# Window attention and a 3x3 convolution on one core: the projection's matmul operands and the path of the softmax reciprocals

## The chip, the cores and the metric

One core of one Trainium2 chip. The metric is the device time of one execution, in microseconds. The kernel before has a median of 3646.91 us over 3 runs (3644.57 to 3647.12).

## The reference

The input is x, 32 images of 56 x 56 positions with 128 channels, fp32. Two residual blocks follow each other:

```python
x = x + L0(_gn(x), qkv_weight, qkv_bias, proj_weight, proj_bias, rel_pos_table)
x = x + L1(_gn(x), w, pruning_mask)
```

_gn is a group norm over 32 groups of 4 channels. L0 is shifted window attention: the image is rolled by 3 positions and cut into 8 x 8 windows of 7 x 7 = 49 tokens; q, k and v are made for 8 heads of 16 channels; the scores get a bias by relative position (and a mask in the windows at the edges); softmax over 49 tokens; times v; then the projection

```python
attn = jax.nn.softmax(attn, axis=-1)
x = jnp.einsum('whnm,whmd->whnd', attn, v).transpose(0, 2, 1, 3).reshape(B * nW, N, C)
x = x @ proj_weight.T + proj_bias
```

L1 is a 3 x 3 convolution, 128 to 128 channels, with binarized weights. All is fp32 in the reference.

## The kernel before, in words

**Layout.** Channels lie on the 128 partitions. An image is worked on in 8 rows of windows (ROWS); a row has 8 windows of 49 tokens, 392 tokens in all (RT). The four pairs of heads (PAIRS) of a row are four units, so an image has 32 units (UNITS), and the kernel has 32 x 8 = 256 rows and 1024 units.

**The order of work.** There is no planner: each engine's program is written out, `for i in images: for u in range(32)`, with fixed places (units) for every job: VALUES_AT = 5, NORMED_AT = 8, SPLIT_AT = 9, PROJ_AT = 9 and so on, plus multiples of 4 for each next row. An engine runs its own list strictly in order and waits on semaphores. Attention of image i, the convolution of image i-1 and the loading and first norm of image i+1 run interleaved in the same loop.

**One unit of attention.** PE computes scores (L908) for a pair of heads; DVE adds the bias (L766, s_sb) and takes the maximum (L771); POOL subtracts it (L443); ACT takes Exp (L498, probs); PE transposes (L919, two units later); ACT copies the result from PSUM (L505, probsT). With all four units of a row there, PE runs the value matmuls (L932), and with head_ones the sums of the probabilities (L936), into attn_ps; both are written column group by column group. These come at unit 5 of a row.

**The reciprocals.** The sums lie 98 columns wide (two windows of 49) on partition 16 h + 4 a + copy, for head h, window pair a (SUM_PARTS = 4) and four equal copies. At unit 6 DVE takes the reciprocal (L746). SP then sends the 32 rows with copy 0 to DRAM (L366, recip_dram), waits for it to land, and reads them back so that each head's 392 values reach its 16 channels' partitions (L371, recip_wide). At unit 8 DVE multiplies (L751, o_sb). SP's queue holds also the loads of x (L378, x_in) and the stores (L383, out_dram).

**The split and the projection.** ACT makes oT_hi, o_sb in fp16 (L548, unit 8, before q in ACT's queue). DVE makes oT_lo = o_sb - oT_hi in fp16 (L759, at the head of unit 9, before that unit's bias add). PE multiplies at the end of unit 9 with the helper `three` (L895): hi x hi, hi-weight x lo, lo-weight x hi, into misc_ps, just before the next row's value matmuls. DVE then adds the result to x (L809) and takes norm statistics (L815). misc_ps is one PSUM bank, shared by the projection, the transposes of x in (L975) and out (L981) and the group norm's small matmuls (L992, fp32, 128 x 128 weights with 2 columns).

qkv (L895 also), with fp16 halves, and the convolution (L1014) use the same high and low scheme; the change leaves them.

Of the kernel before, what the change touches and what calls it, by code (L numbers as in the profile page):

```python
# [31 lines left out]
ALU = mybir.AluOpType  # L32
ACT = mybir.ActivationFunctionType
AX = mybir.AxisListType
F32 = mybir.dt.float32
F16 = mybir.dt.float16
# [37 lines left out]
VALUES_AT, NORMED_AT, SPLIT_AT = 5, 8, 9  # L74
# [88 lines left out]
def build_block(nc, x, wqkv, bqkv, wproj, bproj, table, wconv, prune, ident_d, group_d, parity_d, mask_d, out):  # L163
    with ExitStack() as ctx:
        def sb(name, shape, dt=F32):
            return ctx.enter_context(nc.sbuf_tensor(name, shape, dt))
# [21 lines left out]
        wT_hi = sb("wT_hi", [128, 4, C], F16)  # L188
        wT_lo = sb("wT_lo", [128, 4, C], F16)
# [38 lines left out]
        oT_hi = sb("oT_hi", [128, WIN, W], F16)  # L228
        oT_lo = sb("oT_lo", [128, WIN, W], F16)

        recip_dram = nc.dram_tensor("recip_dram", (2, HEADS, RT), F32).ap()
# [52 lines left out]
        recip_out, recip_wide_in = sem("recip_out"), sem("recip_wide_in")  # L284
        o_ready = sem("o_ready")
        oT_hi_ready, oT_lo_ready = sem("oT_hi_ready"), sem("oT_lo_ready")
# [47 lines left out]
        def _(sp):  # L334
# [24 lines left out]
            def body(i):  # L359
                for u in range(UNITS):  # L360
                    row = row_of(i, u, VALUES_AT + 1)
                    if row is not None:

                        sp.wait_ge(recip_ready, row + 1)
                        need(sp, recip_wide_in, 16 * (row - 1))
                        sp.dma_start(recip_dram[row % 2].rearrange("h (a n) -> (h a) n", a=SUM_PARTS),  # L366
                                     recip[0:128:4, :]).then_inc(recip_out, 16)
                        need(sp, o_ready, row)
                        sp.wait_ge(recip_out, 16 * (row + 1))
                        slot = recip_dram[row % 2]  # L370
                        sp.dma_start(recip_wide[:], bass.AP(tensor=slot.tensor, offset=slot.offset,  # L371
                                                            ap=[[RT, HEADS], [0, HD], [1, RT]]))\
                            .then_inc(recip_wide_in, 16)
# [116 lines left out]
        def _(act):  # L490
# [35 lines left out]
            def body(i):  # L526
                for u in range(UNITS):
# [15 lines left out]
                    row = row_of(i, u, NORMED_AT)  # L543
                    if row is not None:

                        act.wait_ge(o_ready, row + 1)
                        need(act, oT_lo_ready, row)
                        nc.scalar.copy(flat(oT_hi), flat(o_sb)).then_inc(oT_hi_ready, 1)  # L548
# [47 lines left out]
        def _(dve):  # L596
# [49 lines left out]
            step(vec.tensor_copy(w_f[:, 3, :], misc_ps[:, 0:C]))  # L646
            step(vec.tensor_copy(wT_hi[:], w_f))
            step(vec.tensor_tensor(wT_lo[:], w_f, wT_hi[:], ALU.subtract))
# [89 lines left out]
            def body(i):  # L738
                for u in range(UNITS):

                    row = row_of(i, u, VALUES_AT + 1)
                    if row is not None:

                        dve.wait_ge(attn_ready, row + 1)
                        need(dve, recip_out, 16 * row)
                        vec.reciprocal(recip[:], attn_ps[:, RT:RT + SUM_COLS]).then_inc(recip_ready, 1)  # L746
                    row = row_of(i, u, NORMED_AT)
                    if row is not None:

                        dve.wait_ge(recip_wide_in, 16 * (row + 1))  # L750
# [4 lines left out]
                    row = row_of(i, u, SPLIT_AT)  # L755
                    if row is not None:

                        dve.wait_ge(oT_hi_ready, row + 1)
                        vec.tensor_tensor(flat(oT_lo), flat(o_sb), flat(oT_hi), ALU.subtract).then_inc(oT_lo_ready, 1)  # L759
# [114 lines left out]
        def _(pe):  # L874
# [94 lines left out]
            def misc(i, u, kind, t):  # L969
# [12 lines left out]
                if kind == "proj":  # L982
                    pe.wait_ge(oT_lo_ready, i * ROWS + (t + 1 if u >= PROJ_AT else t + 1 - ROWS))
                    hi, lo = (o[:].rearrange("p r w -> p (r w)") for o in (oT_hi, oT_lo))
                    last = three(misc_ps[:, 0:RT], ((wT_hi[:, 3, :], hi), (wT_hi[:, 3, :], lo), (wT_lo[:, 3, :], hi)))
# [109 lines left out]
```

## Time and profile before

| | us |
|---|---|
| median of 3 runs | 3646.91 |
| the profiled execution | 3636.98 |
| its span, first to last instruction | 3635.2 |
| PE busy | 3190.5 (88%) |
| DVE busy | 3073.1 (85%) |
| ACT busy | 2555.1 (70%) |
| POOL busy | 2365.1 (65%) |

The span is the time between the first and the last instruction of the execution that the profiler recorded. Busy shares are of that span. PE is TensorE's matmuls, whose ends are modelled; PEld is its weight loads, which run beside them. SP issues DMAs, and SPq is its queue. An idle time is put down to the instruction or DMA whose semaphore came last. The granted clock of TensorE was 0.983 of full speed over the span.

### The profile page before, as it was taken

What the parts mean: (1) busy time and instruction counts of PE and PEld (TensorE: products, weight loads), DVE (VectorE), ACT (ScalarE), POOL (GpSimd) and SP (SyncE); (2) the same over time, 40 slices, a digit from 0 to 9 for tenths busy, and PEclk for the clock granted to TensorE, in tenths of its full rate; (3) what the DMA queues carried; (4) which work ended last, traced back from release to release, by engine and by line L of the source; (5) the groups of instructions that cost most, each with busy time, mean ns of one, the idle gap of its engine ahead of it and who ended that gap; (6) DMA issues with size and microseconds to landing.
All of it is one profiled execution on the core that took longest, in us unless ns stands there. A gap on an engine that the chain in (4) does not pass through costs nothing.

```text
span 3635.2 us, 155064 instructions
## 1 busy us (share of the span) xinstructions
PE 3190.5 (88%) x64395; PEld 2684.8 (74%) x64395; DVE 3073.1 (85%) x6399; ACT 2555.1 (70%) x5729; POOL 2365.1 (65%) x3683
## 2 busy tenths in 40 slices
PE   2889989889899899898899999889898899898896
PEld 1667777777777777777777777777777777787775
DVE  5689888888888888888888888888888898888895
ACT  1667777767677777777777777777677777777772
POOL 4466666766667666667766667766667666667763
PEclk9999999999999999999999999999999999999998
DMA  2111111111111111111111111111111111111111
GB/s 57 37 42 52 47 42 47 49 50 49 37 47 50 49 52 47 42 47 50 52 52 50 42 45 49 50 52 50 37 47 50 50 52 47 42 47 50 34 35 36
DMA packets 260489, 169.26 MB, mean 47 GB/s; under 512 B 23120, under 2 KB 259792, under 8 KB 259792
## 3 DMA queue, kind: packets, MB, share of 16 engines
q1 hardware_dynamic: 259792, 159.34, 15.9%
q8 instruction: 514, 8.42, 1.0%
q14 instruction: 183, 1.50, 0.1%
HBM read 104.69 MB, written 54.59 MB: 44 GB/s over the span
## 4 chain that ended last, share of the span: by engine, by line
PE 33%; DVE 32%; issue 13%; POOL 9%; DMA 8%; ACT 4%; SPq 0%; DVEq 0%; ACTq 0%; POOLq 0%
PE conv_ps L1014 8%; DVE s_sb L766 6%; PE qkv_ps L895 6%; DMA recip_wide<-recip_dram 5%; PE attn_ps L932 4%; PE scores_ps L908 4%; PE attn_ps L936 4%; DVE plane_lo L778 3%; POOL s_sb L443 3%; DVE s_max L771 3%; DMA recip_dram<-recip 3%; DVE oT_lo L759 3%; PE probsT_ps L919 3%; DVE tok_lo L856 3%; DVE recip L746 2%
## 5 line engine op out<-in xcount | busy, mean ns | idle before, releaser
L443 POOL TENSOR_TENSOR s_sb<-s_sb,s_max 113x392 f32<-113x392 f32 x1024 | 998.9, 975 | 1092.7 <-DVE s_max L771 1091.4
L505 ACT COPY probsT<-probsT_ps 128x392 f32<-128x392 f32 x1024 | 490.8, 479 | 376.6 <-PE probsT_ps L919 366.4
L498 ACT ACTIVATE probs<-s_sb 113x392 f32<-113x392 f32 x1024 | 552.4, 539 | 221.1 <-POOL s_sb L443 218.6
L470 POOL TENSOR_TENSOR plane<-x_n 128x224 f32<-128x224 f32 x896 | 656.4, 753 | 18.7
L919 PE MATMUL probsT_ps<-ident,probs 113*128 113x113 f32 x4096 | 585.0, 265 | 38.7 <-ACT probsT L505 35.3
L771 DVE TENSOR_REDUCE s_max<-s_sb 113x8 f32<-113x392 f32 x1024 | 574.9, 561 | 35.3
L766 DVE TENSOR_TENSOR s_sb<-scores_ps,bias 113x392 f32<-113x392 f32 x1024 | 565.8, 552 | 41.0 <-PE scores_ps L908 37.1
L569 ACT COPY v<-qkv_ps 64x256 f32<-64x256 f32 (+2 forms) x1280 | 391.0, 325 | 211.6 <-PE qkv_ps L895 205.5
L1014 PE MATMUL conv_ps<-plane_hi,wc_hi 128*128 128x224 f16 x2688 | 484.4, 263 | 23.1 <-DVE conv_y L840 19.0
L919 PEld LDWEIGHTS probsT_ps<-ident,probs 113*128 113x128 f32 x4096 | 433.5, 141 | 90.7 <-ACT probs L498 47.9
L908 PE MATMUL scores_ps<-k,q 32*49 32x98 f32 x16384 | 477.4, 252 | 19.7 <-issue 19.4
L1014 PE MATMUL conv_ps<-plane_hi,wc_lo 128*128 128x224 f16 x2688 | 479.4, 261 | 0.0
L1014 PE MATMUL conv_ps<-plane_lo,wc_hi 128*128 128x224 f16 x2688 | 410.1, 262 | 34.9 <-DVE plane_lo L778 34.9
L908 PEld LDWEIGHTS scores_ps<-k,q 32*49 32x49 f32 x16384 | 365.6, 121 | 90.4 <-issue 32.6
L895 PE MATMUL qkv_ps<-wT_hi,tok_hi 128*128 128x128 f16 (+1 forms) x2304 | 395.6, 226 | 3.7 <-ACT v L569 1.9
L895 PE MATMUL qkv_ps<-wT_hi,tok_lo 128*128 128x128 f16 (+1 forms) x2304 | 389.1, 220 | 1.7 <-issue 1.7
L895 PE MATMUL qkv_ps<-wT_lo,tok_hi 128*128 128x128 f16 (+1 forms) x2304 | 389.1, 220 | 0.4 <-issue 0.3
L932 PEld LDWEIGHTS attn_ps<-probsT,v 128*32 128x32 f32 x16384 | 208.5, 113 | 218.5 <-ACT probsT L505 190.6
L932 PE MATMUL attn_ps<-probsT,v 128*32 128x49 f32 x16384 | 244.8, 213 | 129.7 <-ACT probsT L505 128.8
L482 POOL TENSOR_SCALAR x_n<-x,gn_y,gn_shift 128x371 f32<-128x371 f32 (+2 forms) x576 | 347.4, 613 | 7.6 <-POOL gn_shift L432 7.6
L746 DVE RECIPROCAL recip<-attn_ps 128x98 f32<-128x98 f32 x256 | 195.7, 765 | 162.9 <-PE attn_ps L936 162.6
L560 ACT ACTIVATE k<-qkv_ps,k_bias,k_scale 128x392 f32<-128x392 f32 x512 | 322.9, 687 | 4.5 <-PE qkv_ps L895 4.4
(144 smaller groups left out, 6799.1 us busy)
## 6 DMA issues: line engine op xcount, KB each, us to landing
x_in<-in_x_dram SPq DMA_DIRECT2D x224, 224.0 KB, 3.9
recip_wide<-recip_dram SPq DMA_DIRECT2D x256, 196.0 KB
out_dram<-x_out SPq DMA_DIRECT2D x224, 224.0 KB, 2.3
recip_dram<-recip SPq DMA_DIRECT2D x256, 12.2 KB, 1.7
x<-in_L_conv_w_dram SPq DMA_DIRECT2D x1, 576.0 KB
x<-L_conv_pruning_mask_dram SPq DMA_DIRECT2D x1, 576.0 KB
x_n<-_conv_rel_pos_table_dram SPq DMA_DIRECT2D x14, 10.7 KB
x_n<-in_mask_dram SPq DMA_DIRECT2D x1, 196.0 KB
```

The lines of the kernel that those rows point to most:

```text
L443: nc.gpsimd.tensor_tensor(s, s, top, ALU.subtract).then_inc(sub_ready, 1)
L470: last = nc.gpsimd.tensor_tensor(plane[:, t % 2, j], *sums[j])
L498: nc.scalar.activation(probs[0:QP, slot % 2, :, :, 0:N], s_sb[0:QP, slot % 4], ACT.Exp)\
L505: nc.scalar.copy(probsT[:, g % PT_SLOTS], probsT_ps[:].rearrange("p (w n) -> p w n", n=ODD)[:, :, 0:N])\
L569: last = nc.scalar.copy(v[half, slot, w0:w0 + n, :, e * HD:(e + 1) * HD], vals[half, b:b + n, :, e, :])
L766: vec.tensor_tensor(s_sb[0:QP, u % 4].rearrange("p w h m -> p (w h m)"), scores_ps[0:QP, u % 2, 0:WP * 2 * N], bias[0:QP, edge, u % PAIRS] ...
L771: vec.tensor_reduce(s_max[0:QP, u % 4], s_sb[0:QP, u % 4].rearrange("p w h m -> p (w h) m"), AX.X, ALU.max).then_inc(max_ready, 1)
L895: last = mm(out_ps, w, t, start=(n == 0), stop=(n == 2))
L908: last = mm(scores_ps[p0:p0 + N, (u + n) % 2, (w // 2) * 2 * N:(w // 2 + 1) * 2 * N], q[at, r % 2, w, :], k[at, r % 2, w].rearrange("p e m ...
L919: last = nc.tensor.transpose(probsT_ps[:, w * 128:w * 128 + QP], probs[0:QP, u % 2, w].rearrange("p e m -> p (e m)"), ident[0:QP, 0:QP])
L932: mm(attn_ps[parts, w * N:(w + 1) * N], v[:, row % 2, w, pair, :], probsT[:, (row * PAIRS + pair) % PT_SLOTS, w, :], start=True, stop=True)
L1014: last = mm(conv_ps[:, j, 0:PP].rearrange("p (r w) -> p r w", w=W), w[:, j * KW + dx, :], p[:, j, k * TPAIRS:(k + 1) * TPAIRS, dx:dx + W], ...
```

## The change

The fp16 halves of the attention output (oT_hi, oT_lo) are gone, with ACT's and DVE's instructions for them and their semaphores. The projection is one matmul of fp32 weights (w_proj) with o_sb; it waits for o_ready where it waited for oT_lo_ready, at the same place of PE's program. The DRAM tensor for the reciprocals and the DMA into it are gone. In their place four DMAs, one for each window pair a, read recip on the 8 partitions 4 a + 16 h, each with a step of 0 and a count of 16, and write 98 columns of all 128 partitions of recip_wide. SP waits before them for the reciprocal and for o_sb of the row before. DVE's reciprocal waits for the four DMAs of the row before where it waited for the DMA to DRAM. The once-only setup casts three weight matrices to fp16 halves where it cast four.

```diff
--- before.py
+++ after.py
@@ -71,7 +71,7 @@
 
 
 LAG_T = 2
-VALUES_AT, NORMED_AT, SPLIT_AT = 5, 8, 9
+VALUES_AT, NORMED_AT = 5, 8
 MID, END = 0, 1
 PROJ_AT = 9
 G2_JOBS = ((6, END), (7, MID))
@@ -185,8 +185,9 @@
         parity = sb("parity", [128, 2])
         three_halves, zero = sb("three_halves", [128, 1]), sb("zero", [128, 1])
         b_in = sb("b_in", [128, 4])
-        wT_hi = sb("wT_hi", [128, 4, C], F16)
-        wT_lo = sb("wT_lo", [128, 4, C], F16)
+        wT_hi = sb("wT_hi", [128, 3, C], F16)
+        wT_lo = sb("wT_lo", [128, 3, C], F16)
+        w_proj = sb("w_proj", [128, C])
         head_ones = sb("head_ones", [128, SUM_PARTS, 2 * HD])
         w_max = sb("w_max", [128, 4])
         w_inv = sb("w_inv", [128, 4])
@@ -225,10 +226,6 @@
         recip = sb("recip", [128, SUM_COLS])
         recip_wide = sb("recip_wide", [128, RT])
         o_sb = sb("o_sb", [128, WIN, W])
-        oT_hi = sb("oT_hi", [128, WIN, W], F16)
-        oT_lo = sb("oT_lo", [128, WIN, W], F16)
-
-        recip_dram = nc.dram_tensor("recip_dram", (2, HEADS, RT), F32).ap()
 
         class Norm:
 
@@ -281,9 +278,8 @@
         probsT_sb = sem("probsT_sb")
         attn_ready = sem("attn_ready")
         recip_ready = sem("recip_ready")
-        recip_out, recip_wide_in = sem("recip_out"), sem("recip_wide_in")
+        recip_wide_in = sem("recip_wide_in")
         o_ready = sem("o_ready")
-        oT_hi_ready, oT_lo_ready = sem("oT_hi_ready"), sem("oT_lo_ready")
         head_consts = sem("head_consts")
         scaled_bias_ready = sem("scaled_bias_ready")
         tok_hi_ready, tok_lo_ready = sem("tok_hi_ready"), sem("tok_lo_ready")
@@ -362,15 +358,11 @@
                     if row is not None:
 
                         sp.wait_ge(recip_ready, row + 1)
-                        need(sp, recip_wide_in, 16 * (row - 1))
-                        sp.dma_start(recip_dram[row % 2].rearrange("h (a n) -> (h a) n", a=SUM_PARTS),
-                                     recip[0:128:4, :]).then_inc(recip_out, 16)
                         need(sp, o_ready, row)
-                        sp.wait_ge(recip_out, 16 * (row + 1))
-                        slot = recip_dram[row % 2]
-                        sp.dma_start(recip_wide[:], bass.AP(tensor=slot.tensor, offset=slot.offset,
-                                                            ap=[[RT, HEADS], [0, HD], [1, RT]]))\
-                            .then_inc(recip_wide_in, 16)
+                        for a in range(SUM_PARTS):
+                            sp.dma_start(recip_wide[:, a * SUM_COLS:(a + 1) * SUM_COLS],
+                                         recip[SUM_PARTS * a:128:HD, :].unsqueeze(1).to_broadcast((HEADS, HD, SUM_COLS)))\
+                                .then_inc(recip_wide_in, 16)
                     for kind, t in misc_at(i, u):
                         if kind == "tin" and live(i, 2):
 
@@ -540,12 +532,6 @@
                                 .then_inc(m1_ready, 1)
                     if live(i, 0 if u >= LAG_T else -1):
                         evacuate_probsT(i, i * UNITS + (u - LAG_T), u - LAG_T)
-                    row = row_of(i, u, NORMED_AT)
-                    if row is not None:
-
-                        act.wait_ge(o_ready, row + 1)
-                        need(act, oT_lo_ready, row)
-                        nc.scalar.copy(flat(oT_hi), flat(o_sb)).then_inc(oT_hi_ready, 1)
                     misc(i, u, MID)
                     r, j = divmod(u, PAIRS)
                     if live(i, 0 if r < ROWS - 1 else 1):
@@ -643,9 +629,9 @@
             step(vec.tensor_scalar(w_in[:, 3, :], misc_ps[:, 0:C], w_inv[:, 3:4], None, ALU.mult))
             dve.sem_inc(proj_scaled, 1)
             dve.wait_ge(setup_pe, 4)
-            step(vec.tensor_copy(w_f[:, 3, :], misc_ps[:, 0:C]))
-            step(vec.tensor_copy(wT_hi[:], w_f))
-            step(vec.tensor_tensor(wT_lo[:], w_f, wT_hi[:], ALU.subtract))
+            step(vec.tensor_copy(w_proj[:], misc_ps[:, 0:C]))
+            step(vec.tensor_copy(wT_hi[:], w_f[:, 0:3, :]))
+            step(vec.tensor_tensor(wT_lo[:], w_f[:, 0:3, :], wT_hi[:], ALU.subtract))
 
             step(vec.tensor_scalar(q_scale[:], w_max[:, 0:1], HD ** -0.5, None, ALU.mult))
             step(vec.tensor_scalar(q_bias[:], b_in[:, 0:1], HD ** -0.5, None, ALU.mult))
@@ -742,21 +728,16 @@
                     if row is not None:
 
                         dve.wait_ge(attn_ready, row + 1)
-                        need(dve, recip_out, 16 * row)
+                        need(dve, recip_wide_in, 16 * SUM_PARTS * row)
                         vec.reciprocal(recip[:], attn_ps[:, RT:RT + SUM_COLS]).then_inc(recip_ready, 1)
                     row = row_of(i, u, NORMED_AT)
                     if row is not None:
 
-                        dve.wait_ge(recip_wide_in, 16 * (row + 1))
+                        dve.wait_ge(recip_wide_in, 16 * SUM_PARTS * (row + 1))
                         vec.tensor_tensor(o_sb[:].rearrange("p r (w c) -> p w r c", c=WIN),
                                           attn_ps[:, 0:RT].rearrange("p (w r c) -> p w r c", r=WIN, c=WIN),
                                           recip_wide[:].rearrange("p (w r c) -> p w r c", r=WIN, c=WIN), ALU.mult)\
                             .then_inc(o_ready, 1)
-                    row = row_of(i, u, SPLIT_AT)
-                    if row is not None:
-
-                        dve.wait_ge(oT_hi_ready, row + 1)
-                        vec.tensor_tensor(flat(oT_lo), flat(o_sb), flat(oT_hi), ALU.subtract).then_inc(oT_lo_ready, 1)
                     if live(i):
 
                         g = i * UNITS + u
@@ -980,9 +961,8 @@
                     for s in range(SUB):
                         last = nc.tensor.transpose(misc_ps[0:SP_, s * C:(s + 1) * C], result[:, s * SP_:(s + 1) * SP_], ident[:])
                 if kind == "proj":
-                    pe.wait_ge(oT_lo_ready, i * ROWS + (t + 1 if u >= PROJ_AT else t + 1 - ROWS))
-                    hi, lo = (o[:].rearrange("p r w -> p (r w)") for o in (oT_hi, oT_lo))
-                    last = three(misc_ps[:, 0:RT], ((wT_hi[:, 3, :], hi), (wT_hi[:, 3, :], lo), (wT_lo[:, 3, :], hi)))
+                    pe.wait_ge(o_ready, i * ROWS + (t + 1 if u >= PROJ_AT else t + 1 - ROWS))
+                    last = mm(misc_ps[:, 0:RT], w_proj[:], flat(o_sb), start=True, stop=True)
                 if kind in ("gn1", "gn2"):
                     gn, img = (gn1, i + 1) if kind == "gn1" else (gn2, i - 1)
                     if t == 0:
```

## Rows read from the trace of the kernel before

**Rows 1.** The page, part 1: busy us (share of span) and instructions, by engine.

```profile
...
PE 3190.5 (88%) x64395; PEld 2684.8 (74%) x64395; DVE 3073.1 (85%) x6399; ACT 2555.1 (70%) x5729; POOL 2365.1 (65%) x3683
...
```

**Rows 2.** The page, part 4: the chain that ended last, by engine and by line.

```profile
...
PE 33%; DVE 32%; issue 13%; POOL 9%; DMA 8%; ACT 4%; SPq 0%; DVEq 0%; ACTq 0%; POOLq 0%
PE conv_ps L1014 8%; DVE s_sb L766 6%; PE qkv_ps L895 6%; DMA recip_wide<-recip_dram 5%; PE attn_ps L932 4%; PE scores_ps L908 4%; PE attn_ps L936 4%; DVE plane_lo L778 3%; POOL s_sb L443 3%; DVE s_max L771 3%; DMA recip_dram<-recip 3%; DVE oT_lo L759 3%; PE probsT_ps L919 3%; DVE tok_lo L856 3%; DVE recip L746 2%
...
```

**Rows 3.** Waits, whole span: who waited for whom, us in total, times, longest us.

```profile
...
DVE recip L746 <- PE attn_ps L936: 162.6, 105, 4.3
PE attn_ps L932 <- ACT probsT L505: 128.8, 69, 3.4
...
DVE o_sb L751 <- DMA recip_wide<-recip_dram: 103.0, 78, 3.5
DVE x L809 <- PE misc_ps L895: 50.5, 61, 1.5
...
ACT oT_hi L548 <- DVE o_sb L751: 38.6, 75, 8.5
...
PE qkv_ps L895 <- ACT q L557: 26.9, 42, 3.0
...
PE misc_ps L895 <- DVE oT_lo L759: 23.5, 56, 2.6
...
```

**Rows 4.** The chain from 1500 to 1560 us: start us, us, what.

```profile
...
1531.96 0.78 DVE recip L746
1532.76 1.69 DMA recip_dram<-recip
1534.51 4.20 DMA recip_wide<-recip_dram
...
1541.78 0.39 PE probsT_ps L919 x4
...
```

**Rows 5.** Timeline of DVE, 1529 to 1546: start, us, line, shapes, [idle before].

```profile
...
1538.73 0.57 DVE L751 TENSOR_TENSOR o_sb<-attn_ps,recip_wide 128x392 f32<-128x392 f32 x1 [2.18 <-DMA recip_wide<-recip_dram]
...
1541.18 1.20 DVE L759 TENSOR_TENSOR oT_lo<-o_sb,oT_hi 128x392 f16<-128x392 f32 x1
...
```

**Rows 6.** Groups by line and shape: count, busy us, mean ns, idle before.

```profile
...
L759 DVE TENSOR_TENSOR oT_lo<-o_sb,oT_hi 128x392 f16<-128x392 f32 x256 | 223.9, 874 | 2.3 <-ACT oT_hi L548 2.2
...
L548 ACT CAST oT_hi<-o_sb 128x392 f16<-128x392 f32 x256 | 133.2, 520 | 44.5 <-DVE o_sb L751 38.6
...
L992 PE MATMUL misc_ps<-gn_mv,group 128*128 128x2 f32 x128 | 22.1, 242 | 31.2 <-DVE gn_mv L702 16.5 <-ACT x_out L522 12.9 <-DVE gn_mv L706 1.7
...
L992 PEld LDWEIGHTS misc_ps<-gn_mv,group 128*128 128x128 f32 x128 | 19.6, 193 | 38.3 <-ACT x_out L522 19.3 <-issue 18.9
...
```

**Rows 7.** Timeline of PE, 1541 to 1546: the projection.

```profile
...
1543.39 0.33 PE L895 MATMUL misc_ps<-oT_hi,wT_hi 128*128 128x392 f16 x1
1543.56 0.33 PE L895 MATMUL misc_ps<-oT_lo,wT_hi 128*128 128x392 f16 x1
...
```

**Rows 8.** Timeline of PE, same stretch: head_ones matmuls and what follows.

```profile
...
1544.72 0.85 PE L936 MATMUL attn_ps<-probsT,head_ones 128*32 128x98 f32 x32
1545.50 0.72 PE L908 MATMUL scores_ps<-k,q 32*49 32x98 f32 x24
```

**Rows 9.** Timeline of all engines, 1500 to 1516: second DMA and o_sb.

```profile
...
1510.20 0.61 SPq L371 DMA_DIRECT2D recip_wide<-recip_dram  x1
...
1513.50 0.57 DVE L751 TENSOR_TENSOR o_sb<-attn_ps,recip_wide 128x392 f32<-128x392 f32 x1 [0.36 <-DMA recip_wide<-recip_dram]
...
```

**Rows 10.** Timeline of SP, 0 to 14 us: loads at the start.

```profile
...
0.72 0.42 SPq L345 DMA_DIRECT2D ident<-in_ident_dram  x1
1.20 0.41 SPq L345 DMA_DIRECT2D group<-in_group_dram  x1
...
```

**Rows 11.** DMA queues, 1510.2 to 1513.5: packets, MB, share of 16 engines.

```profile
...
q1 hardware_dynamic: 136, 0.20, 18.9%
...
```

**Rows 12.** DMA queues, 1508.4 to 1510.2 us.

```profile
...
q1 hardware_dynamic: 48, 0.01, 3.0%
...
```

## The prediction, made before the changed kernel was run

> **What bounds the kernel now.** I read the engine totals first: in the profiled execution PE is busy 88% of the span, VectorE (DVE) 85%, ScalarE (ACT) 70% [rows 1]. No engine is full, so the second view is the chain of waits: PE holds 33% of the chain, DVE 32%, DMA 8% [rows 2]. PE and DVE carry it by turns. Third, the list of waits says where they hand over [rows 3]. PE stands 128.8 us before the value matmuls (L932) for ScalarE's copy of probsT, and 26.9 and 23.5 us for ACT's q and for DVE's oT_lo. DVE stands 162.6 us before the reciprocal for those same value matmuls, 103.0 us (78 of 256 rows) before o_sb (L751) for the DMA into recip_wide, and 50.5 us before L809 for the projection. The loop over one image row of windows (256 in all, 3635.2 / 256 = 14.2 us each) is: reciprocal, DMA to DRAM, DMA back, o_sb, then at the same place of DVE's queue the scores' bias add and maximum, POOL's subtraction, ACT's Exp and probsT copy, PE's value matmuls, reciprocal. The chain between 1500 and 1560 us shows one pass in which 0.78 us of L746, 1.69 us of the first DMA and 4.20 us of the second follow each other [rows 4]; o_sb then started after 2.18 us in which DVE stood still, and the oT_lo of that row took 1.20 us of DVE one unit on [rows 5].
>
> **The change part by part**, against the profiled execution's own 3636.98 us (span 3635.2; the median of the three runs, 3646.91, is 10 us more, which is added at the end).
>
> *oT_lo on DVE goes.* 256 x 874 ns = 223.9 us of DVE work [rows 6]. The chain names L759 for 3% of the span, 0.03 x 3635 = 109 us [rows 2]; the other 115 us lay beside other work. L759 stands at the head of unit 1 of each row, before that unit's bias add and maximum, so these come earlier, and through POOL and ACT so does the probsT copy for which PE stands 128.8 us. But a little later in the same units DVE waits for PE already (L809 and L746, 50.5 + 162.6 = 213 us [rows 3]): a DVE that arrives earlier waits there unless PE is earlier too. Bounds: -224 us to 0. I take 60% of the chain's 109: **-65 us**, as PE's own waits of 128.8 and 23.5 us are of that size.
>
> *oT_hi on ACT goes.* 256 x 520 ns = 133.2 us of ACT work and 38.6 us of standing for o_sb [rows 3, 6]. It stands before q in ACT's queue, and PE waits 26.9 us for q. The chain's largest lines do not name L548. Bounds -39 to 0; I take a little over half of PE's wait for q: **-15 us**. ACT is the least loaded of the three, so the rest is cover already.
>
> *The projection: three fp16 matmuls become one fp32.* The three start 0.17 us apart (the first two stand in the rows), so they hold PE for 3 x 0.17 = 0.50 us [rows 7]. No full-width fp32 matmul of 392 columns is in the trace. What is there: the 64 gn matmuls (128x128 weights, fp32, two per image) leave 128 records, that is two weight loads (193 ns each) and two matmuls for each, so a full-width fp32 product is run as two [rows 6]. And a moving fp32 column costs two clocks: the 32 head_ones matmuls of 98 columns, four column groups beside each other, hold PE from 1544.72 to 1545.50; 0.78 us / (8 x 98) = 1.0 ns a column; the transposes of 113 columns, four in 0.39 us, 0.86 ns a column [rows 4, 8]. So 2 x 392 x 0.86 = 0.68 us, and of the 193 ns of the first weight load up to 0.1 us more shows than of an fp16 one. Against 0.50 that is +0.18 to +0.28 us a row; I take 0.22, x 256 = **+56 us**, all of it on the path, since with a lighter DVE and ACT it is PE that the others wait for. Bounds: run once like a transpose, 0.34 - 0.50 = -0.16 us a row, -41 us; four times, 4 x 0.34 - 0.50 = +0.86 us, +220 us. I keep the middle as the gn rows are nearest. The result also lands later for L809: a matmul record lasts about 0.16 us beyond its columns, the same as before, so the added wait of DVE is these 0.22 us and not more.
>
> *The two DMAs through DRAM become four from SBUF to SBUF.* Before: from the start of the first issue (1532.76) to that of the second (1534.51) 1.75 us; from there to o_sb, in a row beside no x_in load, 3.3 us (the issue at 1510.20, and at 1513.50 o_sb, which had waited for it) [rows 9]. That is 5.05 us. After: SP issues four in line. The recip_wide issue, which has the same 8 x 16 shape, holds SP 0.61 us, and the start-up loads in one queue follow each other by 0.48 us [rows 9, 10]; so the fourth starts 3 x 0.48 = 1.4 us to 3 x 0.66 = 2.0 us after the first, and I take 2.0. It must then land: the 12 KB DMA took 1.69 us [rows 4], and here 128 packets of 392 B leave on 8 of the 16 engines. (The DMA of 128 rows left 136 packets, 8 beyond its rows, that of 32 rows 48, 16 beyond: one closing packet per engine used [rows 11, 12].) A packet of 392 B took 0.030 x 16 x 1.8 us / 48 = 18 ns, one of 1568 B 0.189 x 16 x 3.3 / 136 = 73 ns; 16 packets per engine are 0.3 us. So 2.0 + 1.7 + 0.3 = 4.0 us, 1.05 us before the old path. Bounds: issues every 0.48 us and a landing of 1.7 us, 3.1 us in all (1.9 us sooner); issues every 0.66 us and a landing as slow as recip_wide's 4.20 us of [rows 4], 6.2 us (1.15 us later). The gain counts only in the 78 rows in which DVE stood for it, and at most what it stood, 1.3 us on average: I take 78 x 0.6 = **-45 us**; bounds -103 and, later by 1.15 us in 78 rows, +90. SP's own queue is no worse: it was held 1.75 + 0.61 = 2.4 us per row by the two steps, and is held 4 x 0.64 = 2.6 us by the four, so x_in and out_dram issues move by 0.2 us, which have units of slack. The reciprocal's new wait is for a DMA that o_sb of the row before has already waited for, so it costs nothing.
>
> The packets argue against splitting only mildly. The Trainium skill (DMA: Bandwidth & Descriptors, Rules for kernel authors) says that small transfers are to be merged, since below 64 KB one pays mostly overhead; the four have 49 KB each, and its fixed cost of some 2 us (section Anatomy of one DMA, given for GpSimd's path), if paid four times in line, makes an estimate of 8 us. The start-up rows [rows 10] show issues every 0.48 us without waiting for the landing, so by this trace the overheads overlap; taken strictly, the rule is the slow rival below.
>
> Sum: -65 - 15 + 56 - 45 = **-69 us**, 3637 - 69 = 3568 for the profiled execution, **3578 us** as a median.
>
> **The rivals.**
> *A: PE takes all.* PE has 3190.5 / 256 = 12.5 us of work in a row of 14.2 [rows 1]. If the waits of DVE and ACT merely swap into waits for PE, the -65 and -15 shrink to the 23.5 us that PE stood for oT_lo, the DMA gain to 20, and +56 stays: about +12 us, 3659 (-20 to +15). For it: the 213 us that DVE already waits for PE. Against it: PE stands 129 us for probsT, behind DVE's work.
> *B: the loop opens.* The issues are short (3.1 us path), the removed L759 stops holding POOL and the fp16 casts, and PE's waits for probsT, q and oT_lo (179 us) all go together with 60 us elsewhere; less 56: -183, about 3465. For it: DMA and DVE lie in one loop. Against it: the 85% of DVE only falls to 79%.
> *C: slower, by the four transfers.* One mechanism: the fourth transfer lands 6.5 us or more after the reciprocal, as the repeated reads of one partition and four closings hold the same 8 engines, worst when an x_in load is in flight. DVE reaches o_sb two units (half a row, 7.1 us) after the reciprocal when nothing holds it; a landing near that makes nearly every row wait. At 7 us: 2 us more than now in 78 rows and 0.5 in half of the others, 156 + 45 = +200, less what DVE's lighter load gives (-80) plus PE's 56: about +176, 3820; at 6.2 us +90 - 80 + 56 = +66, 3713. The decisive point is a landing 0.3 us later than now, at 5.4 us, where 78 x 0.3 cancels the other terms' -24. The same side is reached if the fp32 product runs as four (+220 in place of +56: +95, 3742).
> *That it does not do what it says:* the 8 x 16 repeat could be run as other packets than 128 per DMA; then it is C.
>
> **How the numbers follow.** Chances: forecast (-20 to -130 us) 0.55; A 0.15; B 0.12; C 0.18. The range takes all of the forecast's and part of each rival: 3510 to 3665. 0.2% is 7 us, what this kernel's measurement can tell. Faster: 0.55 + 0.12 + a quarter of A = 0.71; same 0.08, of A; slower 0.18 + the rest of A = 0.21.
>
> **What would show it.** Two records per projection, of some 0.5 us, starting 0.34 us apart; more or fewer refutes that step. SP's four issues with 0.6 us each; the fourth's landing 4.0 us after the first's start. DVE's wait for recip_wide under 60 us in total; no L759, L548; DVE near 2850 us busy; PE's wait for probsT down by a third or more, and DVE's wait for the value matmuls up. If PE's share stays at 88% of a shorter span and probsT's wait is unchanged, the -65 was wrong. If DVE's wait for recip_wide rises, C holds.

## The result, and the profile after

The changed kernel takes 3518.76 us (median of 4 runs, 3518.06 to 3519.10), the kernel before 3645.74 us beside it. The ratio is 0.9659, 95% interval 0.9637 to 0.9681: 3.4% faster, some 124 us. The forecast was 3578 us, in the range 3510 to 3665. The direction and the mechanism's main part came out, with a size 1.8 times that forecast. The kernel before scatters from 3623 to 3658 us over all runs, so the ratios below, each against runs of it beside the kernel, say more than its median; they were run in four groups, in which the kernel before has medians of 3642.7, 3633.9, 3645.9 and 3653.0 us.

The page of the changed kernel, parts 1 and 4, answering to [rows 1] and [rows 2]:

```profile
...
PE 3193.4 (91%) x64139; PEld 2678.4 (76%) x64139; DVE 2897.2 (82%) x6143; ACT 2448.0 (70%) x5473; POOL 2302.2 (65%) x3683
...
```

```profile
...
PE 45%; DVE 21%; POOL 18%; issue 11%; ACT 2%; SPq 1%; DMA 1%; DVEq 0%; POOLq 0%; ACTq 0%
PE conv_ps L994 11%; PE qkv_ps L876 8%; PE scores_ps L889 7%; POOL s_sb L435 6%; PE attn_ps L913 5%; DVE s_sb L747 5%; PE probsT_ps L900 5%; PE attn_ps L917 4%; POOL plane L462 4%; PE misc_ps L965 3%; DVE plane_lo L759 3%; DVE s_max L752 2%; POOL x_n L451 2%; PE misc_ps L956 1%; POOL gn_t L419 1%
...
```

PE has the same busy time in a span 118.9 us shorter: its idle time fell from 3635.2 - 3190.5 = 444.7 us to 3516.3 - 3193.4 = 322.9 us, by 121.8. That is the gain as the page counts it, but not all of its causes: the fp32 product puts 46 us of new work into the 3193.4 us (worked out below), so PE's other work, the same instructions as before, took some 43 us less. Part of that is a higher clock, which e2 below shows. PE went from 33% of the chain to 45%, DVE from 32 to 21, DMA from 8 to 1. DVE's busy time fell by 175.9 us, and not by oT_lo's 223.9 (plane_lo took 14 us more; the rest wasn't traced), to 82%.

The changed kernel's waits, answering to [rows 3] (who waited for whom: us, times, longest us):

```profile
...
DVE recip L732 <- PE attn_ps L917: 196.1, 132, 4.4
DVE x L790 <- PE misc_ps L965: 177.8, 191, 2.6
PE attn_ps L913 <- ACT probsT L497: 143.9, 98, 3.6
...
DVE o_sb L737 <- DMA recip_wide<-recip: 30.4, 44, 2.5
...
PE misc_ps L965 <- DVE gn_mean L697: 16.2, 31, 0.6
...
PE qkv_ps L876 <- ACT q L543: 3.7, 2, 3.0
...
PE scores_ps L889 <- issue: 0.9, 2, 0.5
...
PE conv_ps L994 <- DVE plane_lo L759: 0.9, 1, 0.9
...
PE misc_ps L965 <- DVE o_sb L737: 0.6, 1, 0.6
...
```

Three of these had no row ahead of the prediction. The kernel before has, in the waits of PE:

```profile
...
PE conv_ps L1014 <- DVE plane_lo L778: 34.9, 31, 2.4
PE misc_ps L895 <- DVE gn_mean L711: 30.4, 30, 1.0
...
PE scores_ps L908 <- issue: 19.4, 23, 1.3
...
```

Of PE's 122 us the reader finds 34.0 at the convolution's wait for plane_lo (34.9 to 0.9), 22.9 at the projection's wait for oT_lo (23.5, now 0.6 for o_sb), 23.2 at q (26.9 to 3.7), 18.5 before the scores (19.4 to 0.9) and 14.2 at gn_mean (30.4 to 16.2), 113 us together; two waits for ACT's x_out, 12.9 and 11.1 us, are gone too. The wait for probsT, from which the prediction drew its largest term, did not fall: 128.8 became 143.9 us. DVE's waits for PE grew: before the reciprocal 162.6 to 196.1 us, before L790 (the old L809) 50.5 to 177.8. For recip_wide DVE stands 30.4 us in 44 rows, where it was 103.0 in 78.

The projection and POOL's subtraction by line and form (count, busy us, mean ns, idle before), answering to the rows of L895 and L443:

```profile
...
L435 POOL TENSOR_TENSOR s_sb<-s_sb,s_max 113x392 f32<-113x392 f32 x1024 | 959.9, 937 | 1037.2 <-DVE s_max L752 1036.4
...
L965 PE MATMUL misc_ps<-o_sb,w_proj 128*128 128x392 f32 x512 | 218.6, 509 | 17.9 <-DVE gn_mean L697 16.2 <-ACT x L506 1.2 <-DVE o_sb L737 0.6
...
L965 PEld LDWEIGHTS misc_ps<-o_sb,w_proj 128*128 128x128 f32 x512 | 77.7, 191 | 34.0 <-DVE gn_mean L697 24.3 <-ACT x_out L514 5.7 <-ACT x L506 2.5
...
```

```profile
...
1548.59 0.84 PE L965 MATMUL misc_ps<-o_sb,w_proj 128*128 128x392 f32 x2
1549.36 0.93 PE L913 MATMUL attn_ps<-probsT,v 128*32 128x49 f32 x64
...
```

In the kernel before the three fp16 matmuls start at 1543.39 [rows 7], and the value matmuls at:

```profile
...
1543.98 0.91 PE L932 MATMUL attn_ps<-probsT,v 128*32 128x49 f32 x64
...
```

Each of the 256 projections has two records of some 0.5 us, which start 0.35 us apart (the median of all), and the value matmuls start 0.77 us after the first; before it was 0.59 us. Both figures are also the medians of all rows in which PE did not wait in between. So the product costs PE 0.18 us a row, 46 us.

The four DMAs of one row: the timeline of SP, and the DMA engines from 1511 to 1515 us in 40 slices of 0.1 us (busy tenths, then the queue's packets, MB and share):

```profile
...
1511.05 2.52 SPq L363 DMA_DIRECT2D recip_wide<-recip  x4
...
```

```profile
...
DMA  0000000000000343443334434349343334434320
...
q1 hardware_dynamic: 544, 0.20, 25.8%
...
```

Four issues in 2.52 us, packets from 1.3 to 3.9 us after the first began, 544 = 4 x 136 packets, which by the prediction's count (128 rows and one packet for each engine) is 8 engines again. A packet took 0.258 x 16 x 4 us / 544 = 30 ns. In the 44 rows in which DVE stood for recip_wide, o_sb began 4.2 to 6.0 us after the first issue, 4.3 in the median; before it was 4.9 to 7.6, 5.5 in the median. The path is about 4 us long, as forecast, and some 1.2 us shorter than before.

### The profile page after: what moved, and what is told of

Same layout as the page of the kernel before. It is cut to its first block, busy times and chain, and to the rows that moved or that the text cites. A ratio compares the mean times of both kernels' runs of the same rounds, so it can differ in the third digit from the quotient of the medians.

```text
span 3516.3 us, 154043 instructions
## 1 busy us (share of the span) xinstructions
PE 3193.4 (91%) x64139; PEld 2678.4 (76%) x64139; DVE 2897.2 (82%) x6143; ACT 2448.0 (70%) x5473; POOL 2302.2 (65%) x3683
## 4 chain that ended last, share of the span: by engine, by line
PE 45%; DVE 21%; POOL 18%; issue 11%; ACT 2%; SPq 1%; DMA 1%; DVEq 0%; POOLq 0%; ACTq 0%
PE conv_ps L994 11%; PE qkv_ps L876 8%; PE scores_ps L889 7%; POOL s_sb L435 6%; PE attn_ps L913 5%; DVE s_sb L747 5%; PE probsT_ps L900 5%; PE attn_ps L917 4%; POOL plane L462 4%; PE misc_ps L965 3%; DVE plane_lo L759 3%; DVE s_max L752 2%; POOL x_n L451 2%; PE misc_ps L956 1%; POOL gn_t L419 1%
## 5 line engine op out<-in xcount | busy, mean ns | idle before, releaser
L435 POOL TENSOR_TENSOR s_sb<-s_sb,s_max 113x392 f32<-113x392 f32 x1024 | 959.9, 937 | 1037.2 <-DVE s_max L752 1036.4
L462 POOL TENSOR_TENSOR plane<-x_n 128x224 f32<-128x224 f32 x896 | 639.7, 734 | 18.7
L889 PE MATMUL scores_ps<-k,q 32*49 32x98 f32 x16384 | 458.9, 248 | 0.9 <-issue 0.9
L889 PEld LDWEIGHTS scores_ps<-k,q 32*49 32x49 f32 x16384 | 353.7, 119 | 65.1 <-issue 7.1
L913 PE MATMUL attn_ps<-probsT,v 128*32 128x49 f32 x16384 | 245.7, 214 | 146.2 <-ACT probsT L497 143.9
L732 DVE RECIPROCAL recip<-attn_ps 128x98 f32<-128x98 f32 x256 | 196.2, 766 | 196.3 <-PE attn_ps L917 196.1
L790 DVE SCALAR_TENSOR_TENSOR x<-misc_ps,w_max,x 128x371 f32<-128x371 f32 (+2 forms) x576 | 199.7, 393 | 178.2 <-PE misc_ps L965 177.8
L474 POOL TENSOR_SCALAR x_n<-x,gn_y,gn_shift 128x371 f32<-128x371 f32 (+2 forms) x576 | 333.9, 590 | 7.6 <-POOL gn_shift L424 7.6
```

Of the source, the lines that this page charges most:

```text
L435: nc.gpsimd.tensor_tensor(s, s, top, ALU.subtract).then_inc(sub_ready, 1)
L462: last = nc.gpsimd.tensor_tensor(plane[:, t % 2, j], *sums[j])
L889: last = mm(scores_ps[p0:p0 + N, (u + n) % 2, (w // 2) * 2 * N:(w // 2 + 1) * 2 * N], q[at, r % 2, w, :], k[at, r % 2, w].rearrange("p e m ...
L913: mm(attn_ps[parts, w * N:(w + 1) * N], v[:, row % 2, w, pair, :], probsT[:, (row * PAIRS + pair) % PT_SLOTS, w, :], start=True, stop=True)
```

## The experiments

All times are medians; "of before" is the ratio with its 95% interval.

| run | us | of before |
|---|---|---|
| changed kernel | 3518.8 | 0.9659 (0.9637 to 0.9681) |
| e1: the DMAs alone | 3616.8 | 0.9926 (0.9900 to 0.9952) |
| e3: the fp32 matmul alone, halves still made | 3640.2 | 0.9999 (0.9985 to 1.0012) |
| e2: fp32 matmul, no halves, reciprocals by DRAM | 3532.6 | 0.9702 (0.9675 to 0.9729) |
| e4: changed, subtraction back at its place | 3609.4 | 0.9914 (0.9892 to 0.9936) |
| e8: changed, subtraction late in the unit | 3586.6 | 0.9881 (0.9855 to 0.9907) |
| e9: changed, multiply twice | 3612.9 | 0.9908 (0.9878 to 0.9938) |
| e5: changed, ACT's copy back | 3521.4 | 0.9699 (0.9678 to 0.9720) |
| e6: changed, projection twice | 3625.5 | 0.9982 (0.9968 to 0.9997) |
| e11: changed, tok_lo moved to POOL | 3518.5 | 0.9655 (0.9630 to 0.9680) |
| e10: changed, reciprocals of 49 columns by DRAM | 3654.3 | 1.0025 (1.0008 to 1.0043) |
| e7: changed, projection one unit earlier | 3719.9 | 1.0247 (1.0192 to 1.0301) |
| e12: changed, values and reciprocal first | 3764.9 | 1.0319 (1.0293 to 1.0345) |

### The parts by themselves: e1, e3, e2

e1 is before with SP's four DMAs in place of its two.

> The kernel before with the four SBUF-to-SBUF DMAs alone; the fp16 halves and their three matmuls stay. Theory D (the DMA path carries the gain: DVE's standing for recip_wide fell from 103.0 to 30.4 us, and that loop paces the rows): about 80 us under before, some 3565. Theory V (DVE's removed oT_lo carries it, at the head of unit 1 before the scores' bias add): about 35 us under before, some 3610, and DVE's wait for recip_wide still falls below 40 us.

e3 is before with

```diff
-  last = three(misc_ps[:, 0:RT], ((wT_hi[:, 3, :], hi), (wT_hi[:, 3, :], lo), (wT_lo[:, 3, :], hi)))
+  last = mm(misc_ps[:, 0:RT], w_proj[:], flat(o_sb), start=True, stop=True)
```

> The kernel before with the fp32 matmul in the place of the three fp16 ones; ACT and DVE still make both halves, and PE still waits for oT_lo, though nothing reads them; reciprocals through DRAM. This is the price of the matmul alone. If PE's time there is on the path in full: 0.18 us x 256 = 46 us over before, some 3690. If it is covered by PE's waits for probsT: 0 to +15 us.

e2 is the changed kernel with SP's two DMAs through DRAM.

> The changed kernel with the reciprocals again through DRAM in two DMAs; one fp32 matmul, no halves. Theory V: 90 to 100 us under before, 3545 to 3555, as oT_lo's 224 us of DVE are gone. Theory D: 30 to 50 us under before, about 3605, with DVE's wait for recip_wide at 100 us or more.

The three make a ladder: before 1, the matmul 0.9999, the halves gone 0.9702, the DMAs 0.9659. In us of some 3640: 0, then -108, then -16. The last step is not clear of the noise: the intervals of e2 and of the changed kernel overlap (0.9675 and 0.9681). So theory V holds and D falls. Alone, on the kernel before, the DMAs give 27 us (0.9926; 17 to 36 by the interval). e1's waits show that they did their work and yet gave little:

```profile
...
PE attn_ps L926 <- ACT probsT L499: 143.3, 89, 3.8
...
DVE o_sb L745 <- DMA recip_wide<-recip: 38.7, 39, 2.4
...
```

DVE's wait for recip_wide fell by 64 us, and 14.5 us of it came back as PE's wait for probsT (128.8 to 143.3).

The matmul cost nothing, though it was there. Part 1 of the page of e3, and one of its waits:

```profile
...
PE 3238.2 (89%) x64139; PEld 2703.1 (74%) x64139; DVE 3085.2 (85%) x6400; ACT 2551.0 (70%) x5729; POOL 2360.3 (65%) x3683
...
```

```profile
...
PE attn_ps L934 <- ACT probsT L506: 112.8, 66, 3.1
...
```

PE is 47.7 us busier than before (3238.2 against 3190.5), as 256 x 0.18 = 46 says, in the same time: its idle time gave it, 16 us of that the wait for probsT.

The page of e2, parts 1 and 4, and one of its waits:

```profile
...
PE 3195.7 (90%) x64139; PEld 2678.5 (76%) x64139; DVE 2902.9 (82%) x6143; ACT 2447.9 (69%) x5473; POOL 2300.3 (65%) x3683
...
PE 49%; DVE 21%; issue 9%; POOL 9%; DMA 8%; ACT 3%; SPq 0%; DVEq 0%; ACTq 0%; POOLq 0%
...
```

```profile
...
DVE o_sb L742 <- DMA recip_wide<-recip_dram: 88.4, 76, 3.1
...
```

Here DMA still holds 8% of the chain and DVE stands 88.4 us for recip_wide, and the kernel is only some 15 us slower than the changed one. A wait of 88 us is not a price of 88 us.

Not all of the 108 us between e3 and e2 was waiting. Both run the same 64139 matmuls, and PE is 42.5 us less busy in e2 (3195.7 against 3238.2). Its mean granted clock is higher:

```profile
...
core 0: 3640.2 us, clock 0.979
...
core 0: 3534.0 us, clock 0.988
...
```

(e3, then e2.) The clock has two levels, 1.0 (2.4 GHz) and 0.5 (1.2 GHz), and the mean says how long it stood at the lower one: 2 x 0.021 x 3640 = 153 us in e3, 2 x 0.012 x 3534 = 85 us in e2. At the lower level matmuls take twice as long (rows below), so at most half of the difference, 34 us of the 108, came back with the clock (an estimate). The scatter of one kernel agrees: e1 took 3598.7 us in the run with 0.986 and 3627.6 in one with 0.977. One fall in the kernel before, with the 14 us ahead of it (us, then PE, PEld, DVE, ACT and POOL busy, granted clock, DMA):

```profile
...
977.42:991.42 14.00, 10.23 (x231) 8.05 (x230) 8.93 (x17) 10.08 (x24) 12.41 (x28) 1.00 0.24 67
991.42:994.84 3.42, 3.42 (x19) 1.83 (x20) 2.29 (x5) 2.54 (x6) 3.32 (x5) 0.50 0.02 5
...
```

```profile
...
993.67 0.53 PE L895 MATMUL misc_ps<-oT_hi,wT_hi 128*128 128x392 f16 x1
994.00 0.53 PE L895 MATMUL misc_ps<-oT_lo,wT_hi 128*128 128x392 f16 x1
...
```

PE had been busy for 10.23 of 14.00 us, 73% where its share of the span is 88%, and was then held at the lower level while it worked: the projection's matmuls start 0.33 us apart there, where they start 0.17 us apart at the full clock [rows 7]. Ahead of the other 25 falls between 100 and 3450 us of that trace it was busy 66 to 80%. The kernel before was granted 0.974 to 0.981 in the runs beside these experiments, the changed kernel 0.986 to 0.988; by the same estimate up to some 40 of its 124 us are this. That fewer stalls of PE are what raised the clock fits these traces but is not shown: e7 below has 0.997 with PE 87% busy.

### What the halves cost, put back one at a time: e4, e5, e8, e9

e4 puts on DVE, at the head of unit 9, with nothing waiting for it:

```diff
+  dve.wait_ge(o_ready, row + 1)
+  vec.tensor_tensor(flat(oT_lo), flat(o_sb), flat(oT_hi), ALU.subtract)
```

> The changed kernel with a subtraction of the same shapes as oT_lo (fp16 <- fp32, fp16 of zeros) put back at the head of unit 9 on DVE; nothing waits for it. Theory V: 60 to 90 us over the changed kernel, 3580 to 3610. Theory D: under 20 us over it, 3519 to 3540, since DVE's added work falls into its 178 us of waiting for the projection.

```profile
...
L748 DVE TENSOR_TENSOR oT_lo<-o_sb,oT_hi 128x392 f16<-128x392 f32 x256 | 209.9, 820 | 0.1
...
```

```profile
...
PE 37%; DVE 29%; POOL 19%; issue 13%; ACT 2%; SPq 1%; DMA 0%; DVEq 0%; POOLq 0%; ACTq 0%
...
```

```profile
...
PE attn_ps L921 <- ACT probsT L499: 175.1, 123, 4.0
...
DVE x L798 <- PE misc_ps L973: 86.3, 95, 2.0
...
PE misc_ps L973 <- DVE gn_mean L700: 45.3, 31, 1.7
...
```

e4 costs 0.9914 - 0.9659 = 2.55% of 3640, 93 us (91 by the medians), for 210 us of DVE. DVE is back at 29% of the chain; PE waits 31 us more for probsT and 29 more for gn_mean, while DVE's wait for the projection halves.

e5 puts `nc.scalar.copy(flat(oT_hi), flat(o_sb))` back on ACT in unit 8; nothing reads the copy, and DVE's next o_sb waits for it.

> The changed kernel with ACT's copy of o_sb to fp16 put back at its old place (unit 8, before q), read by nothing. If ACT's removed work was worth what the prediction said: 15 us over the changed kernel, some 3534, with PE's wait for ACT's q back at 20 us or more. If ACT has cover for all of it: 0 to +5 us. If DVE and ACT removals are worth the same per us of work (the subtraction cost 91 us for its 210): 133 us x 0.43 = +57 us.

```profile
...
PE attn_ps L921 <- ACT probsT L499: 120.9, 94, 3.2
...
PE qkv_ps L884 <- ACT q L550: 21.5, 39, 3.0
...
```

PE does wait 21.5 us for q again (3.7 in the changed kernel), but 23.0 us less for probsT (143.9 there), so the wait mostly moved. The kernel takes 2.6 us more by its median, 0.4% by ratios whose intervals touch. So 133 us of ACT work are worth little; the price is between 3 and 15 us.

e8 has e4's subtraction after the projection's take-up, just ahead of the reciprocal's wait.

> As the kernel with the DVE subtraction put back (91 us over the changed one), but it stands at the end of unit 9's list, after the projection is taken up and just before the reciprocal's wait for PE. If its place ahead of the bias add was what it cost: 0 to 25 us over the changed kernel, 3519 to 3545. If DVE's amount of work counts wherever it stands: 70 us or more over it, 3590 and up.

```profile
...
L849 DVE TENSOR_TENSOR oT_lo<-o_sb,oT_hi 128x392 f16<-128x392 f32 x256 | 168.9, 660 | 0.0
...
```

Between the two expectations, near the second: 0.9881, 81 us (68 by the medians) for 169 us of DVE. The place is worth 10 to 20 us of it. The subtraction takes 660 ns here and 820 ns at the head of the unit.

e9 puts a second multiply ahead of o_sb's:

```diff
+  vec.tensor_tensor(o_twin[:].rearrange(...), attn_ps[:, 0:RT].rearrange(...), recip_wide[:].rearrange(...), ALU.mult)
   vec.tensor_tensor(o_sb[:].rearrange(...), attn_ps[:, 0:RT].rearrange(...), recip_wide[:].rearrange(...), ALU.mult)
```

> The changed kernel with o_sb's multiply run once more just ahead of it, from PSUM into a buffer that nothing reads: 560 ns, 143 us of DVE work of a kind that POOL beside it does not stretch (min 550, max 569 ns). The two subtractions put back (210 and 169 us of DVE) cost 0.43 and 0.40 us per us. If DVE's amount of work is what counts: 143 x 0.42 = 60 us over the changed kernel, some 3579. If it was the contention of an fp16-writing subtraction with POOL: under 20 us over, since POOL's mean for its subtraction stays at 937 ns.

```profile
...
L436 POOL TENSOR_TENSOR s_sb<-s_sb,s_max 113x392 f32<-113x392 f32 x1024 | 969.4, 947 | 1144.3 <-DVE s_max L756 1143.2
...
L738 DVE TENSOR_TENSOR o_twin<-attn_ps,recip_wide 128x392 f32<-128x392 f32 x256 | 142.8, 558 | 29.5 <-DMA recip_wide<-recip 28.4 <-DVE gn_y L721 0.4
...
```

91 us (0.9908) for 143 us of DVE, 0.64 us per us, where 60 us were expected. POOL's subtraction stays at 947 ns (937 in the changed kernel), so it was not contention with POOL. Why this operation costs more for each of its us than the two subtractions is not shown; that it stands ahead of o_sb and so also delays the projection is one candidate. The clock has a part in all three: it was granted 0.982 in e4, 0.983 in e8 and 0.979 in e9, where the changed kernel has 0.988. By the estimate made for e2 that is at most 23, 19 and 34 us of their 93, 81 and 91.

### Who paces the changed kernel: e6, e11

e6 runs `mm(misc_ps[:, 0:RT], w_proj[:], flat(o_sb), start=True, stop=True)` twice.

> The changed kernel with the fp32 projection run twice into the same place (same output): 0.68 us more of PE in each of the 256 rows, 174 us. Theory P (PE paces the changed kernel; DVE waits 178 us for the projection already): +150 to +174 us, some 3680. Theory C (PE's standing of 144 us for probsT covers it, as it covered the dearer matmul in the kernel before, which cost nothing): +40 to +90 us, some 3580.

```profile
...
PE 3365.2 (93%) x64651; PEld 2779.7 (77%) x64651; DVE 2898.3 (80%) x6143; ACT 2447.6 (68%) x5473; POOL 2293.8 (63%) x3683
...
PE 56%; DVE 16%; POOL 16%; issue 9%; ACT 2%; SPq 1%; DMA 1%; DVEq 0%; POOLq 0%; ACTq 0%
...
```

```profile
...
DVE x L790 <- PE misc_ps L966: 328.5, 255, 3.2
...
PE attn_ps L913 <- ACT probsT L497: 80.7, 63, 2.9
...
```

Between the theories: 107 us (118 by ratios) for 172 us of PE, 0.62 per us, at an unchanged clock (0.988). The wait for probsT gave 63 us of cover. The same engine's 46 us cost nothing in the kernel before.

e11 moves the block of tok_lo from DVE's list to the end of POOL's, at the same units.

> The changed kernel with tok_lo's subtraction (DVE, 195 us before) moved to POOL, at the end of the same units. If DVE's work is worth 0.42 us per us and POOL, at 65%, takes it in its waits: 80 us under the changed kernel, some 3440. If POOL's order holds up s_sb (POOL is 18% of the changed kernel's chain): slower than it, 3530 to 3600.

```profile
...
PE 3196.9 (91%) x64139; PEld 2683.2 (76%) x64139; DVE 2752.7 (78%) x5887; ACT 2445.4 (70%) x5473; POOL 2478.9 (71%) x3939
...
PE 53%; POOL 17%; DVE 17%; issue 9%; ACT 2%; SPq 1%; DMA 0%; DVEq 0%; POOLq 0%; ACTq 0%
...
```

Neither came: no change (0.9655). DVE is 144.5 us less busy, POOL 176.7 us more, and PE holds 53% of the chain. More DVE work costs the changed kernel 0.4 to 0.64 us per us; less of it, given to POOL, gains nothing. That would fit a kernel at which the bound passes from DVE to PE, as e6 and PE's 53% suggest. But the edit changed two engines: a gain from DVE can have been eaten by POOL's added work, and no run took work from DVE without giving it to another engine.

### Attempts at a faster version: e10, e7, e12

e10 lays the sums out as 64 rows of one window (`SUM_COLS = N; SUM_PARTS = NWIN`) and carries them through DRAM.

> The changed kernel with the sums laid out on 64 partitions of 49 columns (one window each) in place of 32 of 98, and the reciprocals carried through DRAM in two DMAs. DVE's reciprocal halves, some 385 ns or 98 us less DVE work; head_ones runs as 64 short matmuls for 32. If DVE's work is worth 0.42 us per us: 41 us less than the changed projection with DRAM reciprocals (ratio 0.970 to before), so 0.959, and some 20 us under the changed kernel. If what counts is only the place of oT_lo, or PE: no gain, ratio 0.970 or more.

```profile
...
L923 PE MATMUL attn_ps<-probsT,head_ones 128*32 128x49 f32 x16384 | 249.9, 214 | 15.2 <-issue 15.0
...
L738 DVE RECIPROCAL recip<-attn_ps 128x49 f32<-128x49 f32 x256 | 119.8, 468 | 205.9 <-PE attn_ps L923 205.8
...
```

```profile
...
DVE s_sb L753 <- PE scores_ps L895: 163.7, 237, 2.6
...
```

3.3% slower than e2, which it was made from. The reciprocal took 468 ns and not 385, and DVE then waited 163.7 us for scores. PE runs twice the matmuls for the sums: 16384 head_ones records for 8192, and PE's busy time is 63 us above e2's, at a granted clock of 0.980 for e2's 0.988. Half the columns is not half the time on either engine. How the whole 120 us divides was not measured further.

e7 is `PROJ_AT = 8`.

> The changed kernel with PROJ_AT = 8 for 9: the projection runs a unit earlier on PE, and DVE takes it up a unit earlier, which o_sb of unit 8 allows now that no oT_lo is made at unit 9. If DVE's 178 us of standing for the projection pace the rows: 20 to 60 us under the changed kernel, some 3480. If PE then stands for o_sb, or DVE's wait moves one unit up unchanged: 0 to +40 us.

```profile
...
DVE recip L732 <- PE attn_ps L917: 519.6, 253, 5.8
...
PE misc_ps L962 <- DVE x L790: 227.8, 216, 1.4
...
```

Worse than either expectation, 201 us over the changed kernel. DVE's wait for the projection went (5.4 us are left of 177.8), and PE now stood 227.8 us for DVE to empty misc_ps ahead of the output's transposes: with both jobs at the end of the same unit, the one bank of PSUM passes PE, DVE, PE. That held up the value matmuls, and DVE waits 519.6 us for them. At the old place three units lay between a projection and the next transposes of the output. The clock was not the cause, as it was granted 0.997.

e12 exchanges the order in both lists: on PE `values(row)` ahead of the projection, on DVE the reciprocal ahead of the projection's take-up.

> The changed kernel with the value matmuls ahead of the projection in PE's unit, and DVE's reciprocal ahead of its take-up of the projection (all work kept). The reciprocal, the four DMAs and o_sb then start 0.68 us sooner after the scores, and the projection is off that loop. If the changed kernel is paced by PE's amount of work: the same as the changed kernel, ratio 0.963 to 0.968. If it is the loop over the reciprocal (which a multiply added to it lengthened by 94 us for 143): 256 x 0.68 x 0.4 = 70 us under it, ratio about 0.947. If DVE's bias add of the next unit now comes later behind the projection's take-up: slower than it, 0.97 or more.

```profile
...
DVE recip L775 <- PE attn_ps L917: 693.6, 256, 7.8
...
PE attn_ps L913 <- ACT probsT L497: 286.6, 192, 4.3
...
```

The third expectation held, and more strongly than it was put: 3.2% slower than before. DVE now stands at the reciprocal in all 256 rows, 693.6 us; the projection's take-up and the next bias add stand behind it, and with them the probsT for which PE waits 286.6 us. In the old order the take-up lay in that wait. None of the three beats the changed kernel, and e11 equals it.

## Why the prediction was right, point by point

*oT_lo on DVE (-65 us forecast) and oT_hi on ACT (-15):* together 80, measured 108 by e3 to e2. By e5 3 to 15 of it is ACT's, so DVE's term is 93 to 105: undersized by 1.5. Putting the subtraction back costs 93 (e4), which agrees. The step that set it, 60% of the chain's 109 us, since a DVE that comes earlier "waits there unless PE is earlier too", gave DVE's growing waits too much weight. They did grow, by 161 us, but PE was earlier as well. The forecast also has no term for the clock, of which up to 34 us of the 108 may be made. The bound of 224 was safe. The route was partly wrong: probsT's wait was to fall by a third, and it rose by 12%; the gain came at plane_lo, oT_lo, q, the scores and gn_mean, where DVE's and ACT's whole lists run ahead.

*The fp32 matmul (+56 us, "all of it on the path"):* the amount was right, 0.18 us a row by the traces for 0.22, two records each, 0.5 us long and 0.35 us apart. That it was on the path was the step that failed. On the kernel before it cost 0 us (-5 to +4 by e3's interval). This is the largest error of the sum. The rival that PE takes all had PE's share for it, but e3 shows 46 us covered by PE's own 445 us of idle time, even with the halves still made.

*The DMAs (-45 us):* the path was forecast well, 4.0 us (4.3 in the rows that waited) and fewer than 60 us of waiting (30.4). Its 0.66 us for the slowest issue stands in no row; measured were 0.64. The price was too high: 27 us alone and 16 as the last step, neither of them sharp. Counting 0.6 us for each of 78 waiting rows takes a wait for a price; e2 stood 88 us for the DMA and paid 15. The slow rival, by the small transfers, did not appear: four of 49 KB overlapped, and the 8 us that the prediction names for four overheads in line are twice what the trace shows.

So the sum was wrong in three terms that partly offset: 0 for +56, -108 for -80, -16 for -45, in all -124 for -69. Without the +56 the sum would have been -125, because the errors of the other two cancel; that is luck, as it is that the result lies in the stated range, 9 us from its lower end. What was right for its reason is the sign: DVE's removed work carries the gain.

*Rival A (PE takes all)* does not hold for this gain; for a further one e11 and e6 speak for it without deciding it. *Rival B (-183)* had the right mechanism, PE's waits going together, but counted on probsT's wait, which stayed.

What stays open: why PE's wait for probsT doesn't follow DVE's load (128.8 us before, 143.9 in the changed kernel, 141.6 in e11, 175.1 in e4). What decides the granted clock, and so how the gain divides between waits and clock. Also, what the reciprocals by SBUF are worth on a kernel that PE does not pace.

## What to carry to other kernels

In this kernel two engines each held a third of the chain of waits. Work removed from one, DVE, was worth 0.4 to 0.6 of its duration, and work added to the other, PE, cost nothing at first: 224 us less of DVE gave some 100, and the 46 us on PE cost none. After that 172 us more of PE cost 107, and 145 us less of DVE, moved to POOL, gave 0. When a change has two such parts, price the second by a run that makes only that part (e3), not by adding shares of the chain. Look at the granted clock of both kernels before giving the whole difference to waits. And do not move a job only because an engine waits in front of it: both attempts to reorder the jobs (e7, e12) cost over 5% of the changed kernel.

## What the runs showed of the hardware

- A full-width fp32 matmul (128 x 128 weights, 392 columns) runs as two records of some 0.5 us, 0.35 us apart, with a weight load of 190 ns each, and holds PE for 0.77 us up to the next group; three fp16 matmuls of the shape hold it 0.59 us.
- DMAs from SBUF to SBUF whose source repeats a partition 16 times (8 partitions by 16 by 98 fp32) are issued every 0.64 us (four in 2.52 us, the last holding SP for 0.59), use 8 of the 16 engines by the count of packets (136 each), and take 30 ns for a packet of 392 B. The write to DRAM had taken 18 ns for a packet of that size on 16 engines.
- DVE's subtraction from fp32 into fp16 takes 555 to 1209 ns in the kernel before, depending on what POOL does beside it: tok_lo (L856, the same shapes) takes 557 ns in the mean of the 63 rows with POOL idle and 970 in the 127 with POOL busy throughout. Its multiply from PSUM into fp32 stays within 551 to 569.
- DVE's reciprocal from PSUM takes 765 ns for 98 columns and 468 ns for 49.
- TensorE's granted clock falls to its lower level for stretches of some us. At the fall at 991.42 us PE had been 73% busy in the 14 us ahead, and its 392-column fp16 matmuls then started 0.33 us apart for 0.17. The mean does not follow PE's busy share alone: 0.979 at 89% (e3), 0.988 at 91% (changed), 0.997 at 87% (e7).
